# Four of sixteen output products moved behind the last block of a fused linear-attention and mixture-of-depths kernel

## The reference

```python
x = L0_attn_x
xn = _layernorm(x, axis=-1)
x = x + _L0_attn_ref(xn, ...) + _L0_ffn_ref(xn, ...)
```

```python
o = o * jax.lax.rsqrt(jnp.mean(o * o, axis=-1, keepdims=True) + EPS)
o = u * o
return o @ W_out.T
```

```python
_, idx = jax.lax.top_k(scores, k)
...
x1 = x + attn_out
mlp = jax.nn.silu(h2 @ w_gate) * (h2 @ w_up) @ w_down
processed = x1 + mlp
gated = gate * processed + (1.0 - gate) * x
output = hidden_states.at[b, idx].set(gated.reshape(B, k, D))
```

## Time and profile before

| | |
|---|---|
| median of 3 runs | 479.21 us (478.12 to 479.49) |
| profiled execution, its own time | 481.46 us |
| its span, first to last instruction | 479.6 us |
| PE busy | 465.2 us, 97% |
| DVE, ACT, POOL busy | 298.8, 229.5, 192.2 us |
| granted TensorE clock, mean | 0.994 |

### The profile page before, as it was taken

One profiled execution on the slowest core, in us unless ns is written; L12 is line 12 of the kernel. 1 busy time (PEld: TensorE's weight loads), 2 busy tenths in 40 slices (PEclk: granted clock), 3 DMA queues, 4 the chain that ended last, 5 costly groups with the idle time before them and its releaser, 6 DMA issues. The chain is left out here.

```text
span 479.6 us, 11902 instructions
## 1 busy us (share of the span) xinstructions
PE 465.2 (97%) x4839; PEld 422.3 (88%) x4839; DVE 298.8 (62%) x638; ACT 229.5 (48%) x400; POOL 192.2 (40%) x193
## 2 busy tenths in 40 slices
PE   7999999999999999999999998999999999999994
PEld 7988899998998989989899877998888878999993
DVE  6689676887499999755456856767553436230221
ACT  5951243322276779322443436565666446544430
POOL 3240251111120232041367957360470424689862
PEclk9999999999999999999999998999999999999999
DMA  7967675333522111132731689775557822555403
GB/s 227 398 146 123 121 163 85 105 107 110 167 78 68 58 58 55 47 96 65 260 133 46 220 297 326 223 252 176 182 187 274 254 94 88 160 180 186 156 1 44
DMA packets 40951, 72.14 MB, mean 150 GB/s; under 512 B 5872, under 2 KB 7424, under 8 KB 40768
## 3 DMA queue, kind: packets, MB, share of 16 engines
q1 hardware_dynamic: 40352, 70.06, 47.8%
q0 software_dynamic: 544, 1.31, 1.5%
HBM read 54.03 MB, written 17.32 MB: 149 GB/s over the span
## 5 line engine op out<-in xcount | busy, mean ns | idle before, releaser
L1178 POOL TENSOR_TENSOR wlo<-raw,whi 128x512 fp32r<-128x512 f32 x96 | 124.6, 1330 | 88.5 <-ACT whi L564 88.5
L1252 PE MATMUL banks<-HTh,whi 128*128 128x256 f32 x224 | 65.1, 290 | 0.5 <-DVE rope L922 0.4
L1254 PE MATMUL banks<-HTh,wlo 128*128 128x256 f32 x224 | 63.4, 283 | 0.0
L1253 PE MATMUL banks<-HTl,whi 128*128 128x256 f32 x224 | 63.3, 283 | 0.0
L842 DVE TENSOR_TENSOR A<-banks,DEC 128x512 f32<-128x512 f32 x64 | 39.7, 684 | 29.8 <-PE banks L1325 28.3
L1157 POOL TENSOR_TENSOR state_dec<-state,small 128x128 f32<-128x128 f32 x16 | 8.4, 527 | 114.9 <-DVE state L853 114.9
L564 ACT ACTIVATE whi<-raw 128x2048 fp32r<-128x2048 f32 x24 | 45.8, 1908 | 13.2 <-PE banks L1254 7.2
L1252 PEld LDWEIGHTS banks<-HTh,whi 128*128 128x128 f32 x224 | 42.9, 191 | 2.2 <-issue 1.7
L1253 PEld LDWEIGHTS banks<-HTl,whi 128*128 128x128 f32 x224 | 42.9, 192 | 0.3
L1254 PEld LDWEIGHTS banks<-HTh,wlo 128*128 128x128 f32 x224 | 42.9, 191 | 0.0
L1305 PE MATMUL banks<-xTh,WUh 128*128 128x256 f32 x128 | 37.6, 294 | 0.3 <-DVE WUl L787 0.3
(11 more groups left out here) (242 smaller groups left out, 1282.6 us busy)
## 6 DMA issues: line engine op xcount, KB each, us to landing
X<-in_x SPq DMA_DIRECT2D x16, 256.0 KB, 5.8
xn_all<-XN SPq DMA_DIRECT2D x16, 256.0 KB, 6.9
uo_all<-park_h SPq DMA_DIRECT2D x16, 256.0 KB, 2.3
uo_all<-park_l SPq DMA_DIRECT2D x16, 256.0 KB, 3.0
raw<-in_wq SPq DMA_DIRECT2D x4, 1024.0 KB, 6.8
uoh<-uo_all SPq DMA_DIRECT2D x16, 256.0 KB, 3.0
uol<-uo_all SPq DMA_DIRECT2D x16, 256.0 KB, 3.5
XR<-in_x SPq DMA_DIRECT2D x16, 256.0 KB, 3.6
```

The lines of the kernel that those rows point to most:

```text
L1178: ins = Q.tensor_tensor(low[:, k, :], raw[b % 3][:, k, :], high[:, k, :].bitcast(f32), ALU.subtract)
L1252: T.matmul(dst, lh, rh, start=first, stop=False)
L1253: T.matmul(dst, lh, rl, start=False, stop=False)
L1254: return T.matmul(dst, ll, rh, start=False, stop=last)
```

## The change

Tiles 9, 10 and 11 become the `late_outs`. Tiles 12 to 15 become `last_outs`: TensorE multiplies them behind D3, into four banks of their own. So `out_steps` keeps nine steps. Steps 1, 3, 5 and 8 lose their output product, and the nine that stay are for tiles 0 to 8.

The rows of the last four tiles go another way than before. In stage 3, SP loads their x (a fourth `XR` tile is added), ACT runs `base`, and SP writes x + xn alone to `out` (`store_base`). The two scatters then add `delta` to it. SP loads the four tiles back from `out` when the scatters are done (`load_sums`), DVE adds the products (`final`), and SP stores the tiles again.

In chunk 15, `attend` moves ahead of the third unit on TensorE. On ACT the squares, the split of `uo` and the exponential of the gate move ahead of `block_hi(5)` (block K1), and `base(0)` and `base(1)` stand ahead of them all.

```diff
@@ -170,8 +170,8 @@
-        late_outs = (13, 14, 15)
-        out_steps = [0, 1, 2, 3, 4, 5, 7, 8, 10, 11, 12, 13, 14]
+        late_outs, last_outs = (9, 10, 11), (12, 13, 14, 15)
+        out_steps = [0, 2, 4, 7, 10, 11, 12, 13, 14]
@@ -182,6 +182,8 @@
+            if kind == "out" and n in last_outs:
+                return (B[4], B[5], B[0], B[1])[n - last_outs[0]]
             return B[2 + bank_jobs.index((kind, n)) % 2]
@@ -386,13 +398,23 @@
+                elif N == N_TILES - 1:
+                    sp.wait_ge(rope_ok, kq_count(len(units) - 1))
                 else:
                     sp.wait_ge(stored[N % NXR], 16 * (N // NXR))
-                sp.dma_start(XR[N % NXR][:], x_t[N]).then_inc(xr_in[N % NXR], 16)
+                sp.dma_start(rows_of(N)[:], x_t[N]).then_inc(rows_in(N)[0], 16)
...
+            def store_base(N):
+                sp.wait_ge(base_ok, N + 1)
+                sp.dma_start(out_t[N], rows_of(N)[:]).then_inc(base_out, 16)
+
+            def load_sums(N):
+                sp.wait_ge(scattered, 16 * NS), sp.wait_ge(base_out, 16 * len(last_outs))
+                sp.dma_start(rows_of(N)[:], out_t[N]).then_inc(sums_in[N], 16)
@@ -481,6 +503,18 @@
                 if b == block_of["D0"] + 1:
                     for N in late_outs:
                         store(N)
+                    for N in last_outs:
+                        if N < N_TILES - 1:
+                            load_uo(N)
+                        load_x_again(N)
+                if b == block_of["D0"] + 3:
+                    for N in last_outs:
+                        store_base(N)
+            load_uo(N_TILES - 1)
+            for N in last_outs:
+                load_sums(N)
+            for N in last_outs:
+                store(N)
@@ -719,6 +756,9 @@
+                if j == 0:
+                    for N in last_outs:
+                        base(N)
@@ -942,9 +982,11 @@
+                if N in last_outs:
+                    dve.wait_ge(sums_in[N], 16)
@@ -1238,7 +1282,8 @@
-                        pool.wait_ge(stored[c], 16 * len(range(c, N_TILES, NXR)))
+                        pool.wait_ge(stored[c], 16 * len(range(c, last_outs[0], NXR)))
+                    pool.wait_ge(base_out, 16 * len(last_outs))
@@ -1506,11 +1552,13 @@
+                if N == N_TILES - 1:
+                    attend(N)
                 in_position(N, 2)
                 if N >= N_TILES - CH:
                     rms(N - 1)
-                attend(N)
                 if N < N_TILES - 1:
+                    attend(N)
                     new_keys_values(N)
@@ -1600,6 +1648,9 @@
+            pe.wait_ge(sg_ok, 8), pe.wait_ge(pt_ok, FH), pe.wait_ge(ot_lo, FH)
+            for N in last_outs:
+                project_out(N)
```

More of the change, by code:

```diff
@@ L91, in build @@
         tab = at("tab", 140, [P, NS * 2 * FD])
-        XR = [at(f"XR{i}", kb, [P, DM]) for i, kb in enumerate((140, 142, 190))]
+        XR = [at(f"XR{i}", kb, [P, DM]) for i, kb in enumerate((140, 142, 190, 152))]
         HTh, HTl = (at(n, kb, [P, NK, SEL], f32r) for n, kb in (("HTh", 144), ("HTl", 148)))
@@ L278, in build @@
         xa_in, uo_out = (sems(f"{n}_even {n}_odd") for n in ("xa_in", "uo_out"))
-        xr_in, stored, raw_in, ur_in = (sems(f"{n}_0 {n}_1 {n}_2") for n in ("xr_in", "stored", "raw_in", "ur_in"))
+        stored, raw_in, ur_in = (sems(f"{n}_0 {n}_1 {n}_2") for n in ("stored", "raw_in", "ur_in"))
+        xr_in = sems("xr_in_0 xr_in_1 xr_in_2 xr_in_last")
         shead_in, shid_in, wr_in, sbc_in, score_out = sems("shead_in shid_in wr_in sbc_in score_out")
@@ L314, in build, with rows_of, rows_in @@
         down_ps, delta_ok = sems("down_ps delta_ok")
+        def rows_of(N):
+            return XR[N % NXR] if N < N_TILES - 1 else XR[NXR]
+        def rows_in(N):
+            return (xr_in[N % NXR], 16 * (N // NXR + 1)) if N < N_TILES - 1 else (xr_in[NXR], 16)
         def last_use(b):
@@ L586, in uo_high, with base @@
                 S.activation(park_h[:, N % 2], uo[:, N % 2], ACT.Copy).then_inc(uo_hi, 1)
+            def base(N):
+                act.wait_ge(*rows_in(N)), act.wait_ge(gains_ok, 1)
+                S.activation(rows_of(N)[:], rows_of(N)[:], ACT.Identity, scale=gain[:, N:N + 1],
+                             bias=shift[:, N:N + 1]).then_inc(base_ok, 1)
             def in_position(N, position, tiles):
@@ L627, in _ @@
                 in_position(N, 2, tiles)
-                if N >= N_TILES - CH:
+                if N == N_TILES - 2:
                     mean_square(N - 1)
                 if N == N_TILES - 1:
-                    block_hi(5)
+                    base(0)
+                    base(1)
                 if N == 1:
@@ L638, in _ @@
                     uo_high(N)
+                if N == N_TILES - 1:
+                    act.wait_ge(sel_ok, NS)
+                    S.activation(gate, sel_score, ACT.Exp, scale=-1.0).then_inc(gate_exp, 1)
+                    mean_square(N - 1)
+                    block_hi(5)
                 count_marks(ranked(N, 2))
@@ L645, in _ @@
                     block_hi(4)
[L646 to L653, removed]
             def normalised(h):
@@ L684, in _ @@
                     normalised(h)
-                if h in out_at:
+                if out_at.get(h, 0) > 1:
                     base(out_at[h])
@@ L944, in final @@
                 dve.wait_ge(out_ps, N + 1), dve.wait_ge(base_ok, N + 1)
+                if N in last_outs:
+                    dve.wait_ge(sums_in[N], 16)
                 dve.wait_ge(r_ok, 1 + N // (N_TILES // 2))
-                V.scalar_tensor_tensor(out=XR[N % NXR][:], in0=job_bank("out", N)[:], scalar=r_all[:, N:N + 1],
-                                       in1=XR[N % NXR][:], op0=ALU.mult, op1=ALU.add).then_inc(final_ok, 1)
+                V.scalar_tensor_tensor(out=rows_of(N)[:], in0=job_bank("out", N)[:], scalar=r_all[:, N:N + 1],
+                                       in1=rows_of(N)[:], op0=ALU.mult, op1=ALU.add).then_inc(final_ok, 1)
             hs_of = (hs, delta)
@@ L1098, in _ @@
                                        op0=ALU.mult, op1=ALU.add).then_inc(delta_ok, 1)
+            for N in last_outs:
+                final(N)
         @block.gpsimd
@@ L1337, in project_out @@
                 pe.wait_ge(o_w_hi, 1), pe.wait_ge(o_w_lo, 1), pe.wait_ge(ur_in[N % NUO], 32 * (N // NUO + 1))
-                bank_free(("out", N))
+                if N not in last_outs:
+                    bank_free(("out", N))
                 for k in range(NK):
```

7 lines of the change are left out of this document (4 added, 3 removed).

## The result

| | before | changed |
|---|---|---|
| median, 22 runs each | 479.37 us (477.99 to 480.72) | 480.65 us (477.52 to 484.84) |
| profiled execution, its own time | 481.46 us | 481.4 us |
| its span | 479.6 us | 479.7 us |
| granted TensorE clock, mean | 0.994 | 0.992 |

The ratio is 1.0029, with a 95% interval of 1.0015 to 1.0043. The run of 484.84 us is over 1.5% above the fastest of its kernel and is left out of the ratio. The changed kernel is slower by 0.3%. The forecast was 473.9 us, and the range ended at 478.2.

A forecast was written before the change was run, and what follows sets the result against it. TensorE, busy 465.2 of 479.6 us, was taken to bound the kernel. The terms -11.4 - 3.9 + 1.2 + 0 + 8.8 gave -5.3 us, from 479.21 to 473.9 us, range 469.8 to 478.2.

The forecast's parts named there:

- term 4: Stage 3: four `base` on ACT delay G2's rounding, but G2 is just in time: 0 us, bounds 0 and +3.
- rival C: Stage 3 stalls: tile 15's x lands 3 us later, ACT is held, G2 is 3 us late: 476.9 us; chance 0.16.
- Term 3: Heads: new TensorE waits for banks in steps 1, 3 and 5: +1.2 us, bounds 0 and 3.
- Term 1: Heads: four output products leave, the other engines keep up, and TensorE's path shortens by 11.4 us.
- rival A: Heads bound by the chain of exp, rotation and bank; half the removed products' gain lost: 479.6 us; chance 0.08.
- Term 2: Last chunk reordered: waits of 0.42, 0.27 and 1.75 us and 1.34 us of slow clock go: -3.9 us.
- rival D: Reordering brings nothing: idle time and slow clock move to another wait near 285 to 295: 477.8 us; chance 0.08.
- Term 5: The end: four products behind D3, then loads, sums and last store in series: +8.8 us, bounds +7.4 and +16.
- Rival B: End slower than the products: loads and store land in 6.8 us, end costs +16.4: 481.5 us; chance 0.07.

The follow-up runs named there:

- bases_later: Changed kernel with the four `base` of tiles 12 to 15 behind D1's rounding on ACT and their stores behind U3's load: 476.26 us, ratio 0.9917 to the kernel before.
- other_steps: Changed kernel with the heads' output products leaving steps 2, 4, 5 and 8 instead of 1, 3, 5 and 8: 479.96 us, ratio 0.9996 to the kernel before.
- steps_135: `bases_later` with output products in steps 1, 3 and 5, so that they leave 2, 4, 7 and 8: 474.15 us, ratio 0.9890 to the kernel before.
- reorder_alone: Kernel before with only the new order of chunk 15, all sixteen products staying in place: 475.19 us, ratio 0.9903 to the kernel before.
- reorder_again: Same kernel as `reorder_alone`, timed once more in a later group: 475.99 us, ratio 0.9925 to the kernel before.
- move_alone: Changed kernel with chunk 15 in its old order, so only the four products are moved: 484.48 us, ratio 1.0101 to the kernel before.
- no_reload: `bases_later` without `load_sums`: products are added to x + xn still in `XR`, leaving out `delta` for the last four tiles: 474.84 us, ratio 0.9903 to the kernel before.

## Why the prediction was wrong

**The step that failed is term 4**, stage 3 "just in time, at 0 us". In the times of before, which are 12.4 us later there (433.09 against the end of D0 at 420.68), it went like this:

| | forecast | measured + 12.4 |
|---|---|---|
| x of tile 12 issued | 417 | 416.8 |
| x of tile 15 issued | 420.5 | about 420 |
| x of tile 15 landed | 424 | 426.4 |
| `base(15)` done | 424.8 | 427.3 |
| rounding of G2 begins | 426.0 | 428.2 |
| G2's low part ready | 433.1 | 436.0 |

The issue times held; the landing did not. I had taken 3.3 us, the median over all of the kernel's loads of `XR`, for loads that share the queues with six others and with 1 MB right behind. They needed 5.8 (median), and tile 15's, which the sum hung on, 6.4. The other 0.8 us is POOL's part, which ran slower beside DVE. The wait ahead of G2 was thus 3.07 us, rival C's mechanism at its price (+3). The 1.6 us of slow clock behind it stood in no case, though the earlier trace rows show that behind a wait of 1.75 us. `bases_later` shows the cause: with the four `base` one place later the whole 4.8 us are gone. I had written that all of G2's slack was used and each us later cost one us. A term at the edge of its slack should not have been taken at its lower bound.

**Term 3 was undersized**: +1.2 forecast, 4.3 measured (waits of 0.34, 1.94 and 0.69 us and 1.3 us of clock), above its bound of 3. The wait of step 1 was as forecast. The wait of step 3 was 1.94 us where I had 0.3. DVE shows why, in the changed kernel:

```profile
290.56 1.38 DVE L968 TENSOR_TENSOR QR<-rope,rope 128x512 f32<-128x512 f32 x1
291.93 1.18 DVE L1111 TENSOR_SCALAR small<-small 128x2 f32<-128x2 f32 x1
...
293.83 0.48 DVE L959 SCALAR_TENSOR_TENSOR rope<-banks,bqkv,CS 128x256 f32<-128x256 f32 x1
...
295.81 0.98 DVE L962 SCALAR_TENSOR_TENSOR rope<-banks,bqkv,CS 64x256 f32<-64x256 f32 x2
```

The unit of step 3 takes over the bank of step 2's unit, since one product stands between them. TensorE ended step 2's unit at about 291.1, right behind step 1's, with no product in between. So DVE had two rotations to do in a row, and it began the second one only at 293.83; the last instruction that reads the bank began at 295.81 as one of two that took 0.98 us. My layout used the lengths of a step of before, in which DVE was not behind. Two of these rows are also longer than before: the addition into `QR` took 1.38 us in place of 0.69, and the gate's small instruction (128x2) 1.18 in place of 0.16. Both ran while POOL made the low part of a weight block. That is 1.7 us of DVE's time ahead of the second rotation; no run tested it by itself. In `other_steps` and `steps_135` a product stands in step 1 and none in step 2, the unit of step 3 gets the other bank, and this wait is gone. The slow clock behind it is not certain: `bases_later` has the same wait (1.95 us), but the unit behind it took 2.95 us, from 296.75 to 299.70.

**Term 1 held.** The heads took 135.48 us, and with the 3.1 us that term 3 had too little they would have been 132.4, 13.4 less than before; terms 1, 2 and 3 said 13.7. Step 8 ran in 5.89 us, as forecast. Steps 3 and 5 took 8.2 and 6.8 us with their waits, and step 1, which has no work of earlier heads, 4.2. Of rival A a part came true under another name: both engines kept up in steps 8 and 9, but the waits for `rope` in steps 3 and 5 and the clock behind the first are DVE being behind, 3.9 us of the 5.7 that it named.

**Term 2 held.** `reorder_alone` is 3.3 us shorter in the heads, and 0.9903 and 0.9925 are 4.7 and 3.5 us, for -3.9. The two new waits of 1 us were half of rival D; they cost less than what went, and one execution of the two has neither.

**Term 5 held**, 0.9 us better than forecast: +7.9. That is a sum of errors both ways. The scatter landed at T+5.8, 0.7 us sooner. The four loads took 5.6 us to the last landing, where I had 4.7. The last store took 2.0 us from issue, where I had 2.8, and the span ended 0.4 us behind it, where I had 0.9. The Trainium skill (DMA: Bandwidth & Descriptors, "Anatomy of one DMA — SWDGE (gpsimd) path") gives an estimated 4.4 + 2.6 = 7.0 us for loads and store, by a sum fitted to transfers of GpSimd's queue; these are SP's. The trace has 5.6 + 2.0 = 7.6, nearer to my 7.5. It was slower than the page for the four loads together and faster for the one store. Rival B falls: its 6.8 us per step was not reached.

**What lies outside my terms.** Stage 1 was 1.9 us shorter than forecast in the profiled execution of the changed kernel; over all kernels here the first head's scores begin between 279.57 and 282.29 us, with no order by edit; two executions of the same kernel lie 1.4 us apart (`reorder_alone` 281.22, `reorder_again` 279.81). And the profiled execution lay only 0.75 us above its median, where that of before lay 2.1 above, so the medians differ by 1.3 us although the spans differ by 0.1. I have no cause for that. The granted clock of the single runs bears on it. Of the changed kernel's runs, ten of those in the ratio had 0.991 to 0.993 and a median of 482.1 us, ten had 0.995 or 0.996 and 480.1, and one had 0.999 and took 477.52. Of the 17 runs of the kernel before in the first group, six had 0.995 or less, like the profiled execution, with a median of 480.7; the other eleven had 479.6. So how often the clock falls differs between executions of one kernel, and the 1.34 us of slow clock that term 2 took from one trace is probably absent from most runs.

## What to carry to other kernels

An instruction that waits for a transfer holds everything behind it in its engine's list, so ask how long the list behind it can wait; if the answer is "just long enough", move the instruction one place later, for here that was worth 4.8 us. Take a landing time from transfers with the same neighbours in the queues, not from a median over the kernel. When a change has two parts, price and time them apart: here the small one (the order of ten instructions) brought nearly all that the change could bring, and hid that the large one lost.

## What was not expected of the hardware

POOL and DVE took turns. These are DVE's two subtractions into `MT1l` (minimum, median and maximum in ns), one of the same shape with POOL idle, and the two POOL instructions that ran beside the first pair:

```profile
L944 DVE TENSOR_TENSOR MT1l<-staged,MT1h x2: 1373/1583/1793, 418.2 to 419.5; 128x512 fp32r<-128x512 f32 x2
...
405.98 0.68 DVE L944 TENSOR_TENSOR MT0l<-staged,MT0h 128x512 fp32r<-128x512 f32 x1
...
419.00 3.42 POOL L1222 TENSOR_TENSOR wlo<-raw,whi 128x512 fp32r<-128x512 f32 x2
```

Alone DVE's takes 0.68 us and POOL's 1.29. Beside each other DVE's took 1.37 and 1.79, and POOL's 1.75 and 1.72. Each of DVE's ended 0.54 us behind the POOL instruction that was running when it began, and the next of POOL 1.1 to 1.2 us behind DVE's. The Trainium skill (SBUF — State Buffer, "SBUF: two separate sides") says that the two engines share a pair of ports, and that a POOL instruction that reads SBUF, or a DVE instruction with two inputs in SBUF, holds it for its whole length while the other stands. The trace agrees: each waited until the other's had ended. DVE's `staged`, with one input in a bank, took 0.69 us beside POOL as well (427.88 in the kernel before). No run here tested it by itself, but `other_steps` and `move_alone` show the same lengths at this place.

Waits of nearly the same length had different prices. Behind 1.94 us the clock fell for one unit (1.3 us) in the changed kernel; behind 1.95 us in `bases_later` and 1.94 us in `move_alone` and `no_reload` it did not. Behind the wait of 3.1 us ahead of G2 it fell in all three traces that have one. What decides between them the runs don't show.
